# Moving the last third of a layer-norm statistics chain behind the next slab's score products on VectorE

## The chip, the cores and the metric

The kernel runs on the 8 cores of one Trainium2 chip, each with the same program on its own 4096 tokens; no core talks to another. Time is device microseconds of the slowest core.

## What is computed

One transformer layer over 4 sequences of 8192 tokens with 1024 features: an attention in which a token looks at itself and its two neighbours only (16 heads), a layer norm over input plus attention, a mixture of 8 experts of which each token weighs two, and a second layer norm. Cut to what matters here:

```python
xp = x @ Wp.T + bp                       # folded into Wq, Wk, Wv by the kernel
q, k, v = ...                            # 16 heads of 64
scores = einsum('bshd,bsnhd->bshn', q, kn)   # n: the 3 neighbours
attn = softmax(scores); out = einsum('bshn,bsnhd->bshd', attn, vn)
x = layernorm(x + out @ Wo.T + bo)       # (x - mean) / sqrt(var + eps)
x = layernorm(x + moe(x))                # 8 experts, top 2, relu squared
```

## The kernel before

Each core handles its tokens in three stages, one after the other. The first multiplies weight matrices together (to about 215 us). The second, attention and the first layer norm, runs over 8 slabs of 512 tokens (to about 1182 us). The third is the mixture of experts with the second layer norm (the rest). Data lies feature-major: 8 chunks (`dc`) of 128 features on the partitions, 512 tokens along the free axis.

The program is written as one instruction list per engine, with waits on counting semaphores set by hand (`p.wait(engine, semaphore, value)`). An engine executes its list strictly in order, so an instruction that waits holds back all that stand behind it on its engine. `_Prog.do` also puts a drain ahead of an instruction that touches a tile which an earlier one on the same engine has written since the last drain.

The loop over slabs calls these functions in this order (each puts work on several lists):

- `seg_scores(s)`: for each of the 8 chunks VectorE multiplies q with the three shifted k into three of six scratch slots (`pslots`; line 434, 24 products), and TensorE sums each over the features of a head (line 445, four matmuls for three slots, 32 in all). A slot can be written again only when the matmul that read it last is done, so VectorE can run six products ahead of TensorE, no more.
- `seg_softmax_a(s)`: ScalarE takes two exponentials (lines 454, 456); VectorE adds them (line 459).
- `seg_ln1_tail(s - 1)`: TensorE spreads the reciprocal deviation and the mean of the slab before over 128 partitions, reading `stb` (lines 623, 627); ScalarE copies both to slots 2 and 3 (lines 638, 640); VectorE normalises in 16 operations (lines 652, 657); SyncE stores the result.
- `seg_softmax_b(s)`: logarithm and exponential on ScalarE, two products on VectorE (lines 471, 473).
- `seg_qkv(s + 1)`: 384 matmuls (line 401), each group of eight copied out by ScalarE (line 407). Two PSUM banks take turns, so the third group waits for the first copy.
- `seg_wsum(s)`, `seg_wo(s)`: the weighted sum of v and the output projection (lines 493 to 559).
- `seg_ln1_stats_mm(s)`: sums of r1 and of its squares by matmuls with a column of ones (lines 572, 585).
- `seg_xt(s + 2)`: four input tiles are loaded by DMA from GpSimd's queue into two buffers (`xbt`), transposed by TensorE (line 340) and copied out by ScalarE (line 348); then a load of two halo rows and their transpose (line 364). The third and fourth load can start only when a buffer is free again, which is after the transposes of the first and second. This exists for s = 0 to 5.
- `seg_ln1_stats_tail(s)`: on one partition, VectorE computes mean and variance (lines 594 to 600); ScalarE takes the logarithm and the exponential that give 1/deviation (lines 605, 607); VectorE waits for that, multiplies it with the mean and casts both into `stb` (lines 610 to 614).

There is no `seg_qkv` after the scores of the last slab.

On ScalarE's list, lines 605 and 607 stand behind the copies of `seg_xt(s + 2)`. On VectorE's list, lines 610 to 614 stand ahead of the products of `seg_scores(s + 1)`. "Boundary" below is the stretch from the statistics of slab s to the start of `seg_qkv(s + 2)`; there are seven, and the first six hold a `seg_xt`.

Of the kernel before, what the change touches and what calls it, by code (L numbers as in the profile page):

```python
# [98 lines left out]
def build_program(T):  # L99
    assert T % SLAB == 0  # L100
    NSLAB = T // SLAB
# [37 lines left out]
    s_pe = semh("s_pe")  # L139
    s_dve = semh("s_dve")  # L140
    s_act = semh("s_act")
# [3 lines left out]
    p = _Prog(block)  # L145
# [174 lines left out]
    SS = {}  # L320
# [93 lines left out]
    def seg_scores(s):  # L414
        par = s % 2
        v_evac = SS[("evac", s)]
        ps_s[0].wait_writer(p)
        ps_s[2].wait_writer(p)
        si = 0
        vmm = 0  # L420
        for dc in range(NCH):
            prods = {}
            for o in (0, 1, 2):
                slot = si % 6
                si += 1
                scr = pslots[slot]
                if pslot_guard[slot] is not None:
                    p.wait("vector", *pslot_guard[slot])
                p.wait("vector", s_act, max(v_evac[(0, dc)], v_evac[(1, dc)]))
                vv = p.do("vector",  # L430
                          lambda En, o_=scr,
                          a=q_sb[:, par * PB + dc * XFW + 1: par * PB + dc * XFW + 513],
                          b=k_sb[:, par * PB + dc * XFW + o: par * PB + dc * XFW + o + 512]:
                          En.tensor_mul(o_, a, b),
                          reads=[_h(q_sb), _h(k_sb)], writes=[pslot_t[slot]], inc=s_dve)
                prods[o] = (slot, scr, vv)
            for bank, terms in ((ps_s[0], ((0, spk), (1, spkn))),
                                (ps_s[2], ((2, spk), (1, spkn)))):
                for j, (o, stat) in enumerate(terms):
                    slot, scr, vv = prods[o]  # L440
                    p.wait("tensor", s_dve, vv)
                    vmm = p.do("tensor",
                               lambda En, ot=bank.t, l=stat[:, dc * NH:(dc + 1) * NH], r=scr,
                               a=(dc == 0 and j == 0), b=(dc == NCH - 1 and j == 1):
                               En.matmul(ot[0:NH, :], l, r, start=a, stop=b),  # L445
                               inc=s_pe)
                    pslot_guard[slot] = (s_pe, vmm)
        SS[("scores", s)] = vmm

    def seg_softmax_a(s):  # L450
        p.wait("scalar", s_pe, SS[("scores", s)])
        p.wait("scalar", s_act, g_exp)
        p.wait("scalar", s_pe, g_mb)
        p.do("scalar", lambda En: En.activation(sm(0), ps_s[0].t[0:NH, :], AF.Exp),
             reads=[_h(ps_s[0].t)], writes=[_h(smt)], inc=s_act)
        v_e = p.do("scalar", lambda En: En.activation(sm(1), ps_s[2].t[0:NH, :], AF.Exp),
                   reads=[_h(ps_s[2].t)], writes=[_h(smt)], inc=s_act)
        p.wait("vector", s_act, v_e)
        v_sm = p.do("vector", lambda En: En.scalar_tensor_tensor(sm(2), sm(0), 1.0, sm(1), ALU.add, ALU.add),
                    reads=[_h(smt)], writes=[_h(smt)], inc=s_dve)  # L460
        SS[("v_sm", s)] = v_sm
        return v_e
# [127 lines left out]
    def seg_ln1_stats_tail(s):  # L590
        p.wait("vector", s_pe, SS[("v2s", s)])
        p.wait("vector", s_act, g_lnact)
        p.wait("vector", s_pe, SS.get("v_mb", 0))
        p.do("vector", lambda En: En.tensor_scalar_mul(sn(0), ps_s[1].t[0:1, :], 1.0 / D),
             reads=[_h(ps_s[1].t)], writes=[_h(stn)], inc=s_dve)
        p.do("vector", lambda En: En.tensor_scalar_mul(sn(1), ps_st.t[0:1, :], 1.0 / D),
             reads=[_h(ps_st.t)], writes=[_h(stn)], inc=s_dve)
        p.do("vector", lambda En: En.tensor_mul(sn(2), sn(0), sn(0)),
             reads=[_h(stn)], writes=[_h(stn)], inc=s_dve)
        v_var = p.do("vector", lambda En: En.tensor_sub(sn(1), sn(1), sn(2)),  # L600
                     reads=[_h(stn)], writes=[_h(stn)], inc=s_dve)
        ps_s[1].consumed(s_dve, v_var)
        ps_st.consumed(s_dve, v_var)
        p.wait("scalar", s_dve, v_var)
        p.do("scalar", lambda En: En.activation(sn(2), sn(1), AF.Ln, bias=LN_EPS),
             reads=[_h(stn)], writes=[_h(stn)], inc=s_act)
        v_rs = p.do("scalar", lambda En: En.activation(sn(1), sn(2), AF.Exp, scale=-0.5),
                    reads=[_h(stn)], writes=[_h(stn)], inc=s_act)
        p.wait("vector", s_act, v_rs)
        p.do("vector", lambda En: En.tensor_mul(sn(2), sn(0), sn(1)),  # L610
             reads=[_h(stn)], writes=[_h(stn)], inc=s_dve)
        p.do("vector", lambda En: En.tensor_copy(stb[:, 0:512], sn(1)),
             reads=[_h(stn)], writes=[_h(stb)], inc=s_dve)
        v_stb = p.do("vector", lambda En: En.tensor_copy(stb[:, 512:1024], sn(2)),
                     reads=[_h(stn)], writes=[_h(stb)], inc=s_dve)
        SS[("v_stb", s)] = v_stb
        return v_rs

    def seg_ln1_tail(s):
        par = s % 2  # L620
        p.wait("tensor", s_dve, SS[("v_stb", s)])
        ps_s[1].wait_writer(p)
        p.do("tensor", lambda En: En.matmul(ps_s[1].t[:], onescol[0:1, :],
                                            stb[0:1, 0:512], start=True, stop=True),
             inc=s_pe)
        ps_st.wait_writer(p)
        v_mb = p.do("tensor", lambda En: En.matmul(ps_st.t[:], onescol[0:1, :],
                                                   stb[0:1, 512:1024], start=True, stop=True),
                    inc=s_pe)
        SS["v_mb"] = v_mb  # L630
        p.wait("scalar", s_pe, v_mb)
        sbp = pslots[2]
        mbp = pslots[3]
        for sl in (2, 3):
            if pslot_guard[sl] is not None:
                p.wait("scalar", *pslot_guard[sl])
                pslot_guard[sl] = None
        p.do("scalar", lambda En: En.copy(sbp, ps_s[1].t[:]),
             reads=[_h(ps_s[1].t)], writes=[pslot_t[2]], inc=s_act)
        v_bb = p.do("scalar", lambda En: En.copy(mbp, ps_st.t[:]),  # L640
                    reads=[_h(ps_st.t)], writes=[pslot_t[3]], inc=s_act)
        ps_s[1].consumed(s_act, v_bb)
        ps_st.consumed(s_act, v_bb)
        pslot_guard[2] = (s_act, v_bb)
        pslot_guard[3] = (s_act, v_bb)
        p.wait("vector", s_act, v_bb)
        if rstg_free[par] is not None:
            p.wait("vector", *rstg_free[par])
        for dc in range(NCH):
            t0n = pslots[dc % 2]  # L650
            p.do("vector", lambda En, o=t0n, r=r1c(s, dc):
                 En.tensor_mul(o, r, sbp),
                 reads=[_h(q_sb), pslot_t[2]], writes=[pslot_t[dc % 2]], inc=s_dve)
            p.do("vector",
                 lambda En, o=r1n_stg[:, par * NCH * SLAB + dc * SLAB: par * NCH * SLAB + (dc + 1) * SLAB],
                 a=t0n:
                 En.tensor_sub(o, a, mbp),
                 reads=[pslot_t[dc % 2], pslot_t[3]], writes=[_h(r1n_stg)], inc=s_dve)
        g_r1n[par] = s_dve.n
        p.wait("sync", s_hw, s_hw.n)  # L660
        p.wait("sync", s_dve, s_dve.n)
        p.do("sync",
             lambda En, o=r1n_hbm.rearrange("p (c t) -> p c t", t=T)[:, :, s * SLAB:(s + 1) * SLAB],
             i_=r1n_stg[:, par * NCH * SLAB:(par + 1) * NCH * SLAB].rearrange("p (c t) -> p c t", t=SLAB):
             En.dma_start(out=o, in_=i_),
             inc=s_hw, inc_by=16)
        rstg_free[par] = (s_hw, s_hw.n)
# [3 lines left out]
    seg_xt(1)  # L671
    for s in range(NSLAB):
        seg_scores(s)
        v_e = seg_softmax_a(s)
        g_exp = v_e
        if s >= 1:
            seg_ln1_tail(s - 1)
        seg_softmax_b(s)
        if s + 1 < NSLAB:
            seg_qkv(s + 1)  # L680
        seg_wsum(s)
        seg_wo(s)
        seg_ln1_stats_mm(s)
        if s + 2 < NSLAB:
            seg_xt(s + 2)
        v_rs = seg_ln1_stats_tail(s)
        g_lnact = v_rs
        g_mb = s_pe.n
    seg_ln1_tail(NSLAB - 1)

    p.wait("gpsimd", s_pe, s_pe.n)
# [507 lines left out]
```

How the kernel before makes its waits and increments, by code:

```python
    def wait(self, eng, sem, val):  # L39
        if val <= 0:
            return
        self.ops[eng].append(lambda E, s=sem, v=val: E.wait_ge(s.h, v))
# [10 lines left out]
    def do(self, eng, fn, reads=(), writes=(), inc=None, inc_by=1):  # L53
        self._maybe_drain(eng, tuple(reads), tuple(writes))
        if inc is None:
            self.ops[eng].append(lambda E, f=fn: f(E))
        else:
            inc.n += inc_by
            self.ops[eng].append(lambda E, f=fn, s=inc, k=inc_by: f(E).then_inc(s.h, k))
        for h in writes:
            self.dirty[eng].add(id(h))
        for h in reads:
            self.read[eng].add(id(h))
        return inc.n if inc is not None else None
```

## Time and profile before

| | us |
|---|---|
| median of 2 runs | 3712.71 (3698.62 and 3726.8) |
| the profiled execution | 3500.52 |
| its span, slowest core (core 3) | 3499.0 |
| spans of the other cores | 3458.7 to 3491.5 |
| TensorE busy on core 3 | 2817.2 (81%) |
| VectorE busy | 1507.3 (43%) |
| ScalarE busy | 785.2 (22%) |

The profile is of one execution, on its slowest core. PE is TensorE, DVE VectorE, ACT ScalarE, POOL GpSimd, SP SyncE. "<-" in a wait names what ended it. The span runs from the first to the last instruction; the execution's time has 1.5 us more around it.

### The profile page before, as it was taken

What the parts mean: (1) busy time and instruction counts of PE and PEld (TensorE: products, weight loads), DVE (VectorE), ACT (ScalarE), POOL (GpSimd) and SP (SyncE); (2) the same over time, 40 slices, a digit from 0 to 9 for tenths busy, and PEclk for the clock granted to TensorE, in tenths of its full rate; (3) what the DMA queues carried; (4) which work ended last, traced back from release to release, by engine and by line L of the source; (5) the groups of instructions that cost most, each with busy time, mean ns of one, the idle gap of its engine ahead of it and who ended that gap; (6) DMA issues with size and microseconds to landing.
All of it is one profiled execution on the core that took longest, in us unless ns stands there. A gap on an engine that the chain in (4) does not pass through costs nothing.

```text
span 3499.0 us, 43503 instructions; the slowest of 8 cores (3458.7 to 3499.0 us)
## 1 busy us (share of the span) xinstructions
PE 2817.2 (81%) x13600; PEld 1300.6 (37%) x13600; DVE 1507.3 (43%) x2794; ACT 785.2 (22%) x1379; POOL 89.4 (3%) x127
## 2 busy tenths in 40 slices
PE   4578788878886399899967989987889996899992
PEld 1246344434442144344323434432334442344440
DVE  0001534353436344444554444455444455544445
ACT  1133344334433111111121111121111112111111
POOL 1000000000000000000000000000000000000000
PEclk9677888878887699999978999988999996999995
DMA  3420000100000335244324433432623523344431
GB/s 51 61 30 13 13 19 19 25 13 19 19 19 13 80 58 93 49 68 77 56 65 96 72 56 66 73 69 48 124 50 55 91 49 72 73 73 72 69 53 48
DMA packets 98764, 189.71 MB, mean 54 GB/s; under 512 B 3256, under 2 KB 11448, under 8 KB 98544
## 3 DMA queue, kind: packets, MB, share of 16 engines
q0 software_dynamic: 77744, 153.38, 27.0%
q1 hardware_dynamic: 20800, 33.56, 2.8%
q8 instruction: 119, 1.95, 0.2%
q14 instruction: 101, 0.83, 0.1%
HBM read 315.05 MB, written 25.17 MB: 97 GB/s over the span
## 4 chain that ended last, share of the span: by engine, by line
PE 52%; DMA 27%; DVE 8%; issue 5%; ACT 4%; DVEq 2%; ACTq 1%; POOLq 0%; POOL 0%; SPq 0%
PE ps_y L880 16%; PE ps_h L1055 15%; DMA w2e<-w 12%; DMA w1e<-w 11%; PE ps_mm L401 10%; PE ps_mm L551 3%; PE ps_f L225 3%; DMA xbt<-xs 2%; DVEq L49 2%; PE ps_s L445 2%; DVE y_acc L912 1%; ACTq L49 1%; ACT wbe L503 1%; ACT ln2scr L918 1%; DVE ln2t L992 1%
## 5 line engine op out<-in xcount | busy, mean ns | idle before, releaser
L880 PE MATMUL ps_y<-a_sb,w2e 128*128 128x512 bf16 x4096 | 915.6, 385 | 85.4 <-DMA w2e<-w 37.5
L1055 PE MATMUL ps_h<-r1n_ps,w1e 128*128 128x512 bf16 x4096 | 921.5, 386 | 56.9 <-DMA w1e<-w 47.5
L1062 ACT ACTIVATE t1u<-ps_h 128x512 bf16<-128x512 f32 x512 | 305.6, 597 | 1500.8 <-PE ps_h L1055 1453.2
L880 PEld LDWEIGHTS ps_y<-a_sb,w2e 128*128 128x128 bf16 x4096 | 402.8, 99 | 593.0 <-issue 131.2
L1055 PEld LDWEIGHTS ps_h<-r1n_ps,w1e 128*128 128x128 bf16 x4096 | 401.1, 99 | 564.1 <-issue 112.3
L892 DVE TENSOR_TENSOR y_acc<-y_acc,ps_y 128x512 f32<-128x512 f32 x448 | 307.8, 687 | 458.0 <-PE ps_y L880 456.5
L1067 DVE TENSOR_TENSOR t1u<-t1u,ps_gb 128x512 bf16<-128x512 bf16 x256 | 176.1, 688 | 258.1 <-ACT t1u L1062 256.0
L1067 DVE TENSOR_TENSOR t1u<-t1u,ps_b 128x512 bf16<-128x512 bf16 x256 | 176.1, 688 | 178.4 <-ACT t1u L1062 173.1
L1071 DVE TENSOR_TENSOR a_sb<-t1u 128x512 bf16<-128x512 bf16 x512 | 217.7, 425 | 47.7 <-issue 0.9
L225 PE MATMUL ps_f<-wxt_sb,wp_sb 128*128 128x512 bf16 x384 | 103.7, 443 | 84.7 <-DMA wxt_sb<-wqt 48.5
L551 PE MATMUL ps_mm<-k_sb,wot_sb 128*128 128x512 bf16 x512 | 141.6, 444 | 30.6 <-DVE pscr L522 24.2
L519 DVE TENSOR_TENSOR pscr<-wbe,v_sb 128x512 bf16<-128x512 bf16 x64 | 26.9, 420 | 266.8 <-ACT wbe L503 266.8
L401 PE MATMUL ps_mm<-x_fm,ckt 128*128 128x257 bf16 x1024 | 124.4, 284 | 14.2 <-ACT k_sb L407 13.6
L923 PE MATMUL ps_b<-ln2scr,onesv 128*1 128x512 bf16 x64 | 36.8, 576 | 108.1 <-ACT ln2scr L918 108.1
L401 PE MATMUL ps_mm<-x_fm,cvt 128*128 128x257 bf16 x1024 | 121.5, 281 | 0.5 <-ACT v_sb L407 0.2
L401 PE MATMUL ps_mm<-x_fm,cqt 128*128 128x257 bf16 x1024 | 119.1, 277 | 0.3 <-ACT q_sb L407 0.3
L401 PEld LDWEIGHTS ps_mm<-x_fm,ckt 128*128 128x128 bf16 x1024 | 97.5, 101 | 41.7 <-issue 19.3
L401 PEld LDWEIGHTS ps_mm<-x_fm,cvt 128*128 128x128 bf16 x1024 | 96.2, 100 | 24.6 <-issue 1.2
L401 PEld LDWEIGHTS ps_mm<-x_fm,cqt 128*128 128x128 bf16 x1024 | 94.0, 98 | 24.2 <-issue 0.5
L551 PEld LDWEIGHTS ps_mm<-k_sb,wot_sb 128*128 128x128 bf16 x512 | 56.0, 109 | 116.3 <-issue 71.9
L918 ACT CAST ln2scr<-y_acc 128x512 bf16<-128x512 f32 x64 | 39.5, 617 | 254.2 <-DVE y_acc L912 254.2
L225 PEld LDWEIGHTS ps_f<-wxt_sb,wp_sb 128*128 128x128 bf16 x384 | 42.0, 110 | 144.8 <-issue 139.3
(153 smaller groups left out, 1678.6 us busy)
## 6 DMA issues: line engine op xcount, KB each, us to landing
w1e<-w POOLq DMA_DIRECT2D x32, 2048.0 KB, 15.0
w2e<-w POOLq DMA_DIRECT2D x32, 2048.0 KB, 15.2
out<-otok SPq DMA_DIRECT2D x8, 2048.0 KB, 7.2
xbt<-xs POOLq DMA_DIRECT2D x32, 256.0 KB, 3.9
r1n_hbm<-r1n_stg SPq DMA_DIRECT2D x8, 1024.0 KB, 5.2
r1n_ps<-r1n_hbm SPq DMA_DIRECT2D x4, 2048.0 KB, 21.6
wp_sb<-wp POOLq DMA_DIRECT2D x1, 2048.0 KB, 17.1
wxt_sb<-wqt POOLq DMA_DIRECT2D x1, 2048.0 KB, 17.9
```

Source lines behind the costliest of these rows:

```text
L49: self.ops[eng].append(lambda E: E.drain())
L225: En.matmul(o[:], l, r, start=a, stop=b),
L401: En.matmul(o[:, 0:w_], l, r, start=a, stop=b),
L445: En.matmul(ot[0:NH, :], l, r, start=a, stop=b),
L551: En.matmul(o[:], l, r, start=a, stop=b),
L880: En.matmul(o[:], l, r, start=a, stop=b),
L892: va = p.do("vector", lambda En, o=ydst, i_=role.t: En.tensor_add(o, o, i_[:]), reads=[_h(role.t), _h(y_acc)], writes=[_h(y_acc)], inc=s_dve)
L918: vc = p.do("scalar", lambda En, o=rb, i_=ydst: En.copy(o, i_), reads=[_h(y_acc)], writes=[_h(ln2scr)], inc=s_act)
L1055: En.matmul(o[:], l, r, start=a, stop=b),
L1062: va = p.do("scalar", lambda En, o=t1, i_=role.t: En.activation(o, i_[:], AF.Relu), reads=[_h(role.t)], writes=[_h(t1u)], inc=s_act)
L1067: p.do("vector", lambda En, o=u, a=t1, gb_=gbank.t: En.tensor_mul(o, a, gb_[:]), reads=[_h(t1u), _h(gbank.t)], writes=[_h(t1u)], inc=s_dve)
L1071: a=u, b=t1: En.tensor_mul(o, a, b),
```

## The change

`seg_ln1_stats_tail` is cut in two. Its first part ends after the two ScalarE instructions. The second part, `seg_ln1_stats_tail_b`, holds VectorE's wait for them and the three VectorE instructions that form `stb`. It is called after `seg_scores` of the next slab, so on VectorE's list the wait and the three instructions now stand behind the 24 products and ahead of line 459. After the last slab both parts follow each other as before. The new part repeats a wait on the matmuls that last read `stb`. Nothing moves on the lists of TensorE, ScalarE, GpSimd and SyncE.

```diff
--- before.py
+++ after.py
@@ -606,7 +606,12 @@
              reads=[_h(stn)], writes=[_h(stn)], inc=s_act)
         v_rs = p.do("scalar", lambda En: En.activation(sn(1), sn(2), AF.Exp, scale=-0.5),
                     reads=[_h(stn)], writes=[_h(stn)], inc=s_act)
-        p.wait("vector", s_act, v_rs)
+        SS[("v_rs", s)] = v_rs
+        return v_rs
+
+    def seg_ln1_stats_tail_b(s):
+        p.wait("vector", s_act, SS[("v_rs", s)])
+        p.wait("vector", s_pe, SS.get("v_mb", 0))
         p.do("vector", lambda En: En.tensor_mul(sn(2), sn(0), sn(1)),
              reads=[_h(stn)], writes=[_h(stn)], inc=s_dve)
         p.do("vector", lambda En: En.tensor_copy(stb[:, 0:512], sn(1)),
@@ -614,7 +619,6 @@
         v_stb = p.do("vector", lambda En: En.tensor_copy(stb[:, 512:1024], sn(2)),
                      reads=[_h(stn)], writes=[_h(stb)], inc=s_dve)
         SS[("v_stb", s)] = v_stb
-        return v_rs
 
     def seg_ln1_tail(s):
         par = s % 2
@@ -671,6 +675,8 @@
     seg_xt(1)
     for s in range(NSLAB):
         seg_scores(s)
+        if s >= 1:
+            seg_ln1_stats_tail_b(s - 1)
         v_e = seg_softmax_a(s)
         g_exp = v_e
         if s >= 1:
@@ -686,6 +692,7 @@
         v_rs = seg_ln1_stats_tail(s)
         g_lnact = v_rs
         g_mb = s_pe.n
+    seg_ln1_stats_tail_b(NSLAB - 1)
     seg_ln1_tail(NSLAB - 1)
 
     p.wait("gpsimd", s_pe, s_pe.n)
```

## Rows read from the trace of the kernel before

**Rows 1.** the page's head, the slowest core

```profile
span 3499.0 us, 43503 instructions; the slowest of 8 cores (3458.7 to 3499.0 us)
```

**Rows 2.** busy time by stretch: from, to, length, each engine, TensorE clock, DMA, GB/s

```profile
398.00:1182.00 784.00, 596.59 (x3517) 318.15 (x3515) 341.57 (x761) 294.16 (x546) 14.75 (x28) 0.81 0.09 18
...
1182.00:1800.00 618.00, 530.04 (x2340) 228.87 (x2340) 284.04 (x507) 103.02 (x171) 17.17 (x20) 0.93 0.42 74
```

**Rows 3.** TensorE's waits, 280 to 1180 us: us in total, times, longest

```profile
PE ps_s L445 <- DVE pscr L434: 30.2, 7, 7.0
...
PE ps_mm L401 <- ACT k_sb L407: 13.6, 8, 1.9
```

**Rows 4.** VectorE's waits, 280 to 1180 us

```profile
DVE stn L610 <- ACT stn L607: 72.2, 8, 12.6
```

**Rows 5.** timeline around the second slab boundary: start, duration, instruction, [idle before]

```profile
518.54 0.68 DVE L600 TENSOR_TENSOR stn<-stn 1x512 f32<-1x512 f32 x1
...
528.32 0.35 PE L364 MATMUL ps_tb<-idb,xh 2*128 2x2 bf16 x8 [1.57 <-DMA xh<-xs]
...
529.59 0.63 ACT L607 ACTIVATE stn<-stn 1x512 f32<-1x512 f32 x1
530.37 0.68 DVE L610 TENSOR_TENSOR stn<-stn 1x512 f32<-1x512 f32 x1 [11.15 <-ACT stn L607]
...
531.65 0.41 DVE L614 CAST stb<-stn 1x512 bf16<-1x512 f32 x1
531.99 1.78 DVE L434 TENSOR_TENSOR pscr<-q_sb,k_sb 128x512 bf16<-128x512 bf16 x4
...
532.54 0.59 PE L445 MATMUL ps_s<-pscr,spk_sb 128*16 128x512 bf16 x1 [3.88 <-DVE pscr L434]
...
541.52 0.94 DVE L434 TENSOR_TENSOR sqscr<-q_sb,k_sb 128x512 bf16<-128x512 bf16 x2
...
543.13 0.39 PE L623 MATMUL ps_s<-stb,onescol 1*128 1x512 bf16 x1
...
544.56 0.56 ACT L638 CAST pscr<-ps_s 128x512 bf16<-128x512 f32 x1
544.77 0.68 DVE L459 SCALAR_TENSOR_TENSOR smt<-smt 16x512 bf16<-16x512 bf16 x1 [2.31 <-ACT smt L456]
...
546.92 1.01 ACT L407 ACTIVATE k_sb<-ps_mm,cbk 128x257 bf16<-128x257 f32 x2
...
547.52 12.73 PE L401 MATMUL ps_mm<-x_fm,ckt 128*128 128x257 bf16 x112 [1.92 <-ACT k_sb L407]
```

**Rows 6.** stretches inside that boundary, columns as in rows 2

```profile
532.50:537.00 4.50, 4.46 (x11) 1.43 (x12) 3.98 (x11) 0.00 (x0) 0.53 (x1) 0.50 0.41 57
537.00:543.50 6.50, 6.17 (x25) 1.84 (x22) 4.90 (x13) 0.10 (x1) 0.00 (x0) 1.00 0.01 1
```

**Rows 7.** timeline around the seventh boundary, VectorE, then TensorE

```profile
1100.56 0.68 DVE L610 TENSOR_TENSOR stn<-stn 1x512 f32<-1x512 f32 x1 [1.58 <-ACT stn L607]
...
1102.18 1.78 DVE L434 TENSOR_TENSOR pscr<-q_sb,k_sb 128x512 bf16<-128x512 bf16 x4
...
1116.14 0.42 DVE L652 TENSOR_TENSOR pscr<-q_sb,pscr 128x512 bf16<-128x512 bf16 x1 [0.51 <-ACT pscr L640]
...
1102.73 0.58 PE L445 MATMUL ps_s<-pscr,spk_sb 128*16 128x512 bf16 x1 [6.99 <-DVE pscr L434]
...
1125.78 0.58 PE L493 MATMUL ps_s<-wpl,bpk_sb 16*128 16x512 bf16 x1 [11.86 <-DVE wpl L473]
```

**Rows 8.** what TensorE's score products waited for on core 0: us, times

```profile
  DVE pscr L434: 30.4, 8
```

**Rows 9.** POOL's load issues at the second boundary, timeline

```profile
521.85 0.53 POOL L160 DMA_DIRECT2D xbt<-xs  x1 [4.11 <-DMA xbt<-xs]
...
533.68 0.53 POOL L160 DMA_DIRECT2D xbt<-xs  x1 [4.13 <-PE ps_s L445]
```

## The prediction

> **What bounds the kernel now.** I read the page first, to know the size of the whole: a span of 3499.0 us on the slowest core [rows 1], 1.5 us less than that execution's own time of 3500.5 us. Then the busy time by stretch [rows 2]. The reader should see that the attention stage of the loop, 398 to 1182 us, is 784 us long with TensorE busy for 596.6, while the expert stage behind it keeps TensorE busy for 530 of 618 us in its first stretch. The change touches only the attention stage, and there only the places between slabs; all else can only be shifted.
>
> Next the waits of that stage. TensorE's list has one wait that names VectorE's score products: 30.2 us in 7 times, one of them 7.0 [rows 3]. VectorE's has one wait that names the second ScalarE instruction of the statistics: 72.2 us in 8 times [rows 4]. The two are linked, and the timeline of one boundary shows how [rows 5]. VectorE ends line 600 at 518.54 + 0.68 = 519.22 us. It then idles 11.15 us until ScalarE ends line 607. ScalarE is late because its list holds the copies of the next transposes first, and these wait for loads. TensorE ends the last of those transposes at 528.32 + 0.35 = 528.67 us and stands 3.87 us, until the first product arrives for the matmul at 532.54. So what sets the end there is first the loads, up to 528.67, and then a tail in series: lines 605, 607, 610, 612, 614, one product. Only the tail can be taken off. The other five boundaries with a transpose stage repeat this: (30.2 - 7.0) / 6 = 3.87 us each. The 11.15 us of VectorE's idling are no measure of the gain, since TensorE is busy with loads and transposes for most of them.
>
> **What is removed: the six full boundaries.** After the change VectorE goes from 519.22 us straight to the products. Their inputs (q and k of the next slab) were made before the weighted sum, and the slots are free. All 24 took 541.52 + 0.94 - 531.99 = 10.47 us, 0.436 us each [rows 5]. Six fill the slots by about 521.9; VectorE then waits for TensorE, which arrives at 528.67. The first score matmul starts there: 3.87 us earlier.
>
> Does the head start of six products bring more? Before, the last product ended 542.46 - 532.54 = 9.92 us after the first matmul. After, the seventh product needs the first matmul done, the eighth the fourth, and so on round the slots. TensorE issued 11 matmuls in the first 4.5 us, 0.41 each, at a granted clock of 0.50, the lower level of 1.2 GHz, and was at 1.00 after that [rows 6]. Walking the slots at this pace, the thirteenth product starts about 4.65 us after the first matmul, and the last ends 12 x 0.436 = 5.2 later, at 9.9 us. The head start is used up by the slow clock, so I take 0. If the clock rose at once, 18 products from 0.75 us on would end at 8.6: 1.3 us more gain. If it rose a little later than before, some 0.4 less.
>
> **What is added behind the scores.** The three instructions took from 530.37 to 531.65 + 0.41 = 532.06, 1.69 us. They now stand behind the last product. VectorE stood idle there for 2.31 us before line 459 [rows 5], so on VectorE itself they are hidden, with 0.6 us to spare; the wait for line 607 ahead of them is long over (529.59 + 0.63 = 530.22). But `stb` is late next. TensorE's line 623 started 543.13 - 542.46 = 0.67 us after the last product; now it must wait until 0.05 + 1.69 + 0.1 = 1.84 us after it, 1.17 us more, and line 627, the whole of `seg_qkv` and, by line 638, ScalarE are queued behind it. ScalarE's line 638 started 2.10 us after the last product because two exponentials were ahead of it. Now line 627 starts at 1.84 + 0.22 and takes as long as line 623's 0.39, which with some 0.15 of signalling gives 2.6: ScalarE is 0.5 us late, and with it lines 640, 466, 468 and the copy of line 407. TensorE's own 1.17 us mostly vanish, since after 16 matmuls it waited 1.92 us for that copy anyway until 547.52 [rows 3, 5]. Net loss 0.5 us a boundary; bounds 0 (if signalling is quicker) and 1.17 (if nothing absorbs it).
>
> A full boundary gains 3.87 - 0.5 = 3.4 us, bounds 3.87 - 0.4 - 1.17 = 2.3 and 3.87 + 1.3 = 5.2. Six: 20.2 us (14 to 31).
>
> **The seventh boundary** has no transposes. VectorE idled 1.58 us before line 610 and spent 1102.18 - 1100.56 = 1.62 until the first product [rows 7]. Both leave the path, less about 0.1: 3.1 us. TensorE's 6.99 us become 3.9. No projection follows there: the path goes by VectorE's 16 normalising operations from 1116.14 to TensorE's 11.86 us wait that ends at 1125.78, and the first of the 16 waits for ScalarE's copies, late by the same 0.5. Gain 2.6 us (1.9 to 3.1). The last slab's tail is unchanged.
>
> **Sum.** 20.2 + 2.6 = 22.8 us, bounds 16 and 34. Against the profiled execution, 3500.5 - 22.8 = 3477.7. The median of the two runs shown is 3712.7, 212 us above the profiled execution; nothing in the trace says where these lie. The gain is made of VectorE and ScalarE durations, which do not follow TensorE's clock, so I take it off unchanged: 3712.7 - 22.8 = **3689.9 us**, a gain of 0.6%. Core 0 shows the same wait, 30.4 us [rows 8], so the slowest core has no special position.
>
> **The loads.** The products now run while loads are in flight. At 521.85 POOL found its load landed after 4.11 us, which ran beside one-partition work; the load whose landing it awaited until 533.68 took 4.13, beside lines 610 to 614 and four products [rows 9]. I take 0 for it. The Trainium skill speaks against the change here: the page SBUF — State Buffer, section on who interferes with whom, says VectorE and GpSimd share ports under an exclusive lock, and a load issued from GpSimd stalls while VectorE holds it. By that rule the loads would come later by up to the six products; by the row nothing moves.
>
> **The rivals.**
> - *The loads are stretched by the products.* Place: the tile load issued about 517.2. Price: at most the six early products, 2.6 us a boundary, 15.6 us over six. The sum becomes 7 us: 3705.5. Against it the two equal landings; for it, that they are a thin sample. Chance 0.13.
> - *The change does nothing that counts.* Another wait keeps the products where they are, a slot or a late q, or the gain is lost before the projection. Then TensorE's wait stays at 3.87 and the time at 3712.7. The slots' last readers and the copies of q are done long before, so 0.04.
> - *Slower: the clock stays low into the projection.* TensorE starts on the scores after 12 us of sparse transposes, and now meets a second pause of 1.2 us at line 623. Before, the clock had risen 4.5 us into the scores and was 1.00 ahead of the projection [rows 6]. If it stayed at 0.50, each microsecond of the projection's work would take one more. 3.4 us of such work in each boundary cancels the gain, and that is where it decides; 5 us cost 6 x 1.6 = 10 us net of it: 3722. Being 2% slower takes (74 + 23) / 7 = 14 us of it each time. Against it: the 1.92 us pause at 547.52 did not bring the clock down before. Chance 0.07.
>
> **From these to the numbers.** The forecast holds 0.76. The two runs shown lie 14 us either side of their median, and the expert stage's mean clock of 0.93 [rows 2] moves it: 0.01 of it over 2317 us, TensorE busy for 86%, is some 21 us, as much as the whole gain and with no sign of its own. The range goes from the upper bound of the gain less both runs' distance (3712.7 - 34 - 28 = 3651) to the slower rival and a little over it, 3725. About 2% is what a measurement of this kernel can tell from no change, 74 us. No case of the profile reaches that; I leave 0.04 for faster and 0.03 for slower, and 0.93 within.
>
> **What the profile after would show.** VectorE's wait at line 610 falls from 72.2 us to nearly the last slab's 1.6. VectorE's waits at line 434 on TensorE grow instead, by about 7.5 us (521.9 to 528.67 + 0.75) in each of six boundaries. TensorE's wait at line 445 falls from 30.2 to about 4, all in the seventh. TensorE gains a wait at line 623, 7 times 1.2 us, and its wait at line 401 for line 407 shrinks from 1.9 to about 1.3. Scores end about 3.9 us sooner after the transposes. Landing times of the loads stay at 4 us. The prediction is wrong if these landings grow, if the scores end no earlier, or if the first projection matmuls show a clock of 0.50.

## The result

| | before | after |
|---|---|---|
| median, us | 3479.7 (10 runs, 3475.0 to 3749.3) | 3454.1 (11 runs, 3448.8 to 3640.1) |
| ratio | | 0.9927, 95% interval 0.9916 to 0.9939 |
| first to last line 600, us (7 slabs) | 768.3 (core 3), 767.6 (core 7) | 744.0 (core 7) |

The change takes 0.73% off, 25 us (21 to 29). Some executions of either kernel are 4 to 8% longer than the rest, with a lower granted clock on one half of the cores or on both; the ratio compares the shorter ones alone, and the two runs shown ahead of the prediction were both of the longer kind. With the eight runs measured later the median before is 233 us lower. The third row is my yardstick for the attention stage below: from the start of line 600 (the last of VectorE's four statistics operations, whatever number it has in a kernel) in the first slab to the same in the last. It holds all seven boundaries and nothing of the first and last stage. It fell by 23.6 us on core 7 (by 19.9 to 25.0 on the eight cores, core by core), against a forecast of 22.8 for the whole.

The waits of TensorE after the change (slowest core, core 7, same stretch as rows 3, same columns):

```profile
PE ps_tb L340 <- DMA xbt<-xs: 47.5, 12, 4.8
...
PE ps_s L627 <- DVE stb L619: 14.7, 8, 6.8
...
PE ps_mm L401 <- ACT k_sb L407: 10.3, 8, 2.2
...
PE ps_s L445 <- DVE pscr L434: 3.7, 1, 3.7
```

The reader should hold the last line against the first of [rows 3]: 30.2 us in seven waits have become 3.7 in one, which is the seventh boundary. The new line is the wait for `stb`; 6.8 us of it belong to the last slab and were there before, so the change added 7.9 us in seven waits, 1.1 each. Part of that came back: the wait for ScalarE's copy went from 13.6 to 10.3 us. The first line is no gain of the change: core 7 lies some 24 us earlier in its span than core 3 did before, so the stretch cuts off two waits of the first slabs; from 240 us on both kernels wait 55.4 us for tiles, 14 times. VectorE's wait that was 72.2 us [rows 4] is now this (core 7):

```profile
DVE stn L615 <- ACT stn L607: 1.7, 1, 1.7
```

The second boundary in the timeline (core 7, columns as in rows 5, whose lines these answer):

```profile
490.80 0.68 DVE L600 TENSOR_TENSOR stn<-stn 1x512 f32<-1x512 f32 x1
491.41 1.78 DVE L434 TENSOR_TENSOR pscr<-q_sb,k_sb 128x512 bf16<-128x512 bf16 x4
...
501.10 0.35 PE L364 MATMUL ps_tb<-idb,xh 2*128 2x2 bf16 x8 [1.78 <-DMA xh<-xs]
501.44 0.58 PE L445 MATMUL ps_s<-pscr,spk_sb 128*16 128x512 bf16 x1
...
502.20 0.42 DVE L434 TENSOR_TENSOR pscr<-q_sb,k_sb 128x512 bf16<-128x512 bf16 x1 [8.16 <-PE ps_s L445]
...
510.42 0.94 DVE L434 TENSOR_TENSOR sqscr<-q_sb,k_sb 128x512 bf16<-128x512 bf16 x2
...
511.28 0.67 DVE L615 TENSOR_TENSOR stn<-stn 1x512 f32<-1x512 f32 x1
...
512.55 0.41 DVE L619 CAST stb<-stn 1x512 bf16<-1x512 f32 x1
...
513.21 0.37 PE L627 MATMUL ps_s<-stb,onescol 1*128 1x512 bf16 x1 [1.12 <-DVE stb L619]
...
514.00 0.58 ACT L642 CAST pscr<-ps_s 128x512 bf16<-128x512 f32 x1 [0.45 <-PE ps_st L631]
...
516.98 12.73 PE L401 MATMUL ps_mm<-x_fm,ckt 128*128 128x257 bf16 x112 [1.31 <-ACT k_sb L407]
```

VectorE now goes from the statistics to the products without a pause and then stands 8.16 us because its slots are full. TensorE starts the scores with no idle at all behind the last transposes. The last product ends at 511.36, 9.92 us after the first score matmul, exactly as before the change. `stb` then costs what it was to cost: line 627 starts 1.85 us after the last product (0.67 before), line 642 (638 before) 2.64 (2.10 before), and the projection goes on 5.62 us after it (5.06 before).

A table that no single view gives: the time from TensorE's first matmul of one kind to its first of the next, from its timeline, mean over the six full boundaries. It carries most of what follows, so the kernels measured later stand in it too. "Transposes" runs from the first transpose to the first score matmul, with the waits for the loads in it; weighted sum and output projection (wo) are means over the last seven slabs. Each kernel stands with its slowest core, but warm2_after with core 4, since on its cores 2 and 3 the clock was low in the projection (774.9 and 782.7 us in the last column). The cores of one execution differ by up to 9.4 us in the last column, mostly in wo; where that matters, all eight are given.

| kernel | transposes | scores | projection | weighted sum | wo | first to last line 600 |
|---|---|---|---|---|---|---|
| before | 17.1 | 11.3 | 45.5 | 17.6 | 20.1 | 768.3 |
| changed | 13.5 | 12.4 | 44.9 | 17.6 | 19.8 | 744.0 |
| early | 13.2 | 11.3 | 45.6 | 17.6 | 19.8 | 740.6 |
| dbl | 12.7 | 14.0 | 45.9 | 17.6 | 19.3 | 754.2 |
| warm2_after | 13.3 | 10.9 | 45.0 | 17.9 | 18.5 | 728.2 |
| port_mul | 13.1 | 12.6 | 45.0 | 17.6 | 20.0 | 744.9 |
| port_copy | 13.7 | 12.2 | 45.0 | 17.6 | 19.7 | 743.9 |
| bufs4_before | 8.8 | 11.4 | 45.6 | 17.6 | 18.7 | 709.6 |
| bufs4_after | 4.5 | 11.9 | 44.9 | 18.0 | 18.5 | 681.3 |
| bufs4_early | 7.2 | 11.2 | 45.6 | 18.0 | 19.5 | 704.3 |
| bufs4_after_wo | 4.5 | 11.8 | 45.0 | 18.6 | 16.7 | 674.0 |

Before to changed, for one full boundary: 3.6 us less ahead of the scores, 1.1 more in them (TensorE's wait for `stb` counts there), 0.6 less in the projection. The seventh boundary gave 3.3 us in its statistics stage (11.5 to 8.2). Nothing shows that the few tenths in the wo stage are the change's doing; what sets its length is a finding of its own, below.

### The profile page after: what moved, and what is told of

Same layout as the page of the kernel before. It is cut to its first block, busy times and chain, and to the rows that moved or that the text cites. A ratio compares the mean times of both kernels' runs of the same rounds, so it can differ in the third digit from the quotient of the medians.

```text
span 3449.2 us, 43503 instructions; the slowest of 8 cores (3353.9 to 3449.2 us)
## 1 busy us (share of the span) xinstructions
PE 2790.8 (81%) x13600; PEld 1287.7 (37%) x13600; DVE 1507.4 (44%) x2794; ACT 785.7 (23%) x1379; POOL 89.4 (3%) x127
## 4 chain that ended last, share of the span: by engine, by line
PE 53%; DMA 27%; DVE 8%; issue 5%; ACT 4%; DVEq 2%; ACTq 1%; POOLq 0%; POOL 0%; SPq 0%
PE ps_y L887 16%; PE ps_h L1062 15%; DMA w2e<-w 12%; DMA w1e<-w 10%; PE ps_mm L401 10%; PE ps_mm L551 3%; PE ps_f L225 3%; DMA xbt<-xs 2%; DVEq L49 2%; PE ps_s L445 2%; DVE y_acc L919 1%; ACT wbe L503 1%; ACT ln2scr L925 1%; ACTq L49 1%; DVE ln2t L999 1%
## 5 line engine op out<-in xcount | busy, mean ns | idle before, releaser
L225 PE MATMUL ps_f<-wxt_sb,wp_sb 128*128 128x512 bf16 x384 | 90.7, 401 | 85.2 <-DMA wxt_sb<-wqt 48.7
L401 PE MATMUL ps_mm<-x_fm,ckt 128*128 128x257 bf16 x1024 | 118.8, 275 | 10.9 <-ACT k_sb L407 10.3
L434 DVE TENSOR_TENSOR pscr<-q_sb,k_sb 128x512 bf16<-128x512 bf16 x128 | 51.5, 422 | 140.0 <-PE ps_s L445 71.5
## 6 DMA issues: line engine op xcount, KB each, us to landing
wp_sb<-wp POOLq DMA_DIRECT2D x1, 2048.0 KB, 17.4
```

The source lines that it names most:

```text
L225: En.matmul(o[:], l, r, start=a, stop=b),
L401: En.matmul(o[:, 0:w_], l, r, start=a, stop=b),
```

## The experiments

The edits are shown shortened, in part in words.

**early: the late stb taken away.**

```diff
 seg_xt(s + 2), on ScalarE's list
     copy of transposed tile 0, copy of tile 1
+    lines 605, 607 (logarithm, exponential) here
     copy of tile 2, copy of tile 3, halo copy
 VectorE, boundaries 1 to 6
+    tail_b ahead of the products, seventh boundary behind them
```

> The changed kernel with ScalarE's two statistics instructions moved ahead of its third transpose copy, where ScalarE stands idle for a load anyway, and VectorE's last three instructions back ahead of the products (the seventh boundary stays as changed). It takes away the cost that the prediction put at 0.5 us a boundary, late stb, and keeps the 3.87. Theory: TensorE's wait for stb goes from 14.7 us to the last slab's 6.8 plus about 1, its wait at the score products stays near 4 us (the seventh boundary alone), and the time from the first to the last line 600 falls from 744.0 to 741 us; ratio 0.992. Rival (moving the chain off ScalarE's list is all that counts, or the 0.5 us was never paid): 744 us, ratio 0.993. Rival on the other side (VectorE now starts its products 3.3 us later, at about 522.5 in the second boundary's time, and that is too late for TensorE): over 745 us.

Measured: 740.6 us, ratio 0.9924 (0.9906 to 0.9942). The interval of the whole kernel can't tell 0.9924 from 0.9927; the stage table can. The scores stage gives back its 1.1 us and the projection takes 0.7 again: 0.4 us a boundary (3.4 us in all by the yardstick), for which the prediction had 0.5. In the medians over the eight cores of each kernel the scores stage gives back 1.4, so 0.7 net; the price of the late stb lies between 0.4 and 0.7 us. TensorE's waits on core 3, the one for stb almost wholly the last slab's again:

```profile
PE ps_s L633 <- DVE stb L625: 8.0, 2, 6.8
...
PE ps_s L447 <- DVE pscr L436: 3.7, 1, 3.7
```

The first product starts later than in the changed kernel, yet TensorE did not wait for it: while the loads last, where VectorE does its three instructions is free.

**dbl: the late stb made later.**

```diff
 def seg_ln1_stats_tail_b(s):
     p.wait("vector", s_act, SS[("v_rs", s)])
     p.wait("vector", s_pe, SS.get("v_mb", 0))
+    if s < NSLAB - 1:
+        two tensor_mul of 1x512 fp32 on a scratch tile
```

> The changed kernel with two more one-partition products (0.68 us each and a drain, together 1.54 us, results unused) ahead of line 615 in the moved part, at the seven boundaries. It doubles the one cost that the prediction added. Theory (late stb is now on the path by way of ScalarE's copies, with nothing left to absorb more of it): the whole 1.54 us is paid at each boundary, 7 x 1.54 = 10.8 us, 744.0 becomes 755 us, ratio 0.996; TensorE's wait for stb grows by 10.8 us. Rival (it hides behind ScalarE and the 0.7 us that VectorE still idles): 744 to 750 us, ratio 0.993 to 0.994.

Measured: 754.2 us against 744.0, ratio 0.9970 (0.9958 to 0.9983), which is 15 us above the changed kernel; TensorE's wait for stb 24.3 us, 9.6 more than in the changed kernel. At its own place the lateness is paid almost in full: in the medians over eight cores the scores stage is 1.45 us longer, and at the seventh boundary the time from the scores to the weighted sum is 1.5 longer, 10.2 us in all of the 10.8 forecast. The total is not so clean. Core by core it grew by 2.3 to 10.2 us: wo was shorter here (18.6 us in the median over the cores, 19.7 in the changed kernel) while the projection was longer in some slabs. The start of one such projection (core 0), then the same one in the changed kernel (core 7), columns as in rows 2:

```profile
967.68:972.58 4.90, 4.02 (x25) 2.81 (x25) 2.60 (x7) 3.16 (x6) 0.00 (x0) 0.64 0.00 0
```

```profile
964.57:969.47 4.90, 3.59 (x32) 2.96 (x32) 3.28 (x8) 3.63 (x7) 0.00 (x0) 1.00 0.00 0
```

This is the prediction's third rival, the clock low into the projection, and it appears when TensorE stands 2.49 us for stb in the place of 1.12: 19 of the 48 projections (six boundaries, eight cores) are 0.9 to 2.4 us longer than the changed kernel's median at the same boundary and 11 more are 0.2 to 0.6 longer, while the changed kernel's own 48 spread by less than 0.3 us. The change stayed clear of it by less than 1.4 us of waiting. With `early` this gives the shape: the first 1.2 us of lateness cost 0.4 to 0.7, because ScalarE's two exponentials and TensorE's wait for ScalarE's copy cover the rest; beyond that nearly all is paid, and in some slabs a slow projection comes on top.

**port_mul and port_copy: do the loads feel VectorE?**

```diff
 seg_scores(s), 1 <= s <= 6, after the sixth product
+    13 x tensor_mul(dmb, cqt[:, 0:512], ckt[:, 0:512])       # port_mul
+     8 x tensor_copy(dmy[:, 0:1024], dmy[:, 1024:2048])      # port_copy, fp32
```

> The changed kernel with VectorE kept busy after its sixth product by 13 more products of two on-chip bf16 tiles (0.52 us each with the drain, results unused), so that it works through the loads of the fourth tile and the halo rows instead of standing idle. Theory (the loads do not feel VectorE): TensorE's waits for xbt and xh stay at 55 and 14 us in all and POOL sees each load land after 4.0 to 4.3 us. Rival (the lock between VectorE and GpSimd's descriptor writing): landings longer by 0.5 to 2 us, the waits 10 to 20 us longer.

> The same with 8 copies of 1024 fp32 elements in the place of the 13 products: single-source copies, the form that the Trainium skill (SBUF, State Buffer, section on who interferes with whom) names as the one that locks GpSimd out. Theory (loads do not feel VectorE): landings 4.0 to 4.3 us, as with the products. Rival (that rule): each copy holds the port for its whole duration, descriptors are written only between copies, and the landings of the fourth tile and the halo rows grow by 1 to 3 us, TensorE's waits by 10 to 30 us in all.

Measured: 744.9 and 743.9 us. From 240 us on, TensorE's waits for tiles and for halo rows are 52.9 and 14.8 us with products (55.4 and 14.6 in the changed kernel on core 7): nothing. With copies they are 55.4 and 15.9, and the issue itself changed. GpSimd's load issues in the view of line 160, first the changed kernel (core 7), then port_copy (core 2; durations as min/median/max ns, then the first and the last start):

```profile
L160 POOL DMA_DIRECT2D xbt<-xs x32: 528/528/557, 198.4 to 944.6; - x32
...
L160 POOL DMA_DIRECT2D xh<-xs x8: 511/511/522, 216.2 to 949.4; - x8
```

```profile
L160 POOL DMA_DIRECT2D xbt<-xs x32: 528/530/988, 195.8 to 941.6; - x32
...
L160 POOL DMA_DIRECT2D xh<-xs x8: 517/682/918, 214.1 to 946.4; - x8
```

The second boundary of port_copy in VectorE's and then in GpSimd's timeline (core 2):

```profile
490.84 6.18 DVE L428 COPY dmy<-dmy 128x1024 f32<-128x1024 f32 x8
```

```profile
490.65 0.99 POOL L160 DMA_DIRECT2D xbt<-xs  x1 [3.77 <-DMA xbt<-xs]
```

An issue that falls among the copies takes up to 0.99 us in the place of 0.53. That fits the lock of which the Trainium skill speaks (SBUF — State Buffer, section on who interferes with whom): copies can shut GpSimd out, while products of two tensors do not hold up a load. Both agree here: no issue among port_mul's took over 0.56 us on any core. The lock costs 0.1 to 0.5 us an issue, not the 1 to 3 that the rival had for a landing, and the time did not follow. So the first rival of the prediction, loads stretched by the products, is out: the change's products do not do it (a tile lands after 3.8 us in the median with and without the change, on core 7), and even the worse form would cost a few tenths.

**warm_before, warm_after, warm2_after: is the head start eaten by the slow clock?** Filler matmuls into a PSUM bank that the scores overwrite later; the numbers are per wait (third tile, fourth tile, halo).

```diff
 seg_xt(s), s >= 2, on TensorE's list ahead of the wait for the load
+    fill(8), fill(7), fill(3)        # warm_*: matmuls 128x512 of idb and cqt
+    fill(14), fill(16), fill(7)      # warm2_after
```

> The changed kernel with filler matmuls on TensorE (8, 7 and 3, results unused) ahead of the waits for the third tile, the fourth tile and the halo rows in the six boundaries that have transposes; they fit into waits of 4.3, 3.6 and 1.7 us. It tests the step that the six products of head start are worth nothing because TensorE reads the scores at the lower clock. Theory (slow clock eats the head start): the score matmuls start at a granted clock of 1.00, the last product ends 8.6 us after the first score matmul instead of 9.9, and the kernel is 6 x 1.3 = 8 us faster than the changed kernel, a ratio of about 0.990 to the kernel before. Rival (VectorE and the slots set the pace whatever the clock): last product still 9.9 us after the first matmul, ratio 0.993. Second rival (fillers get in the way of the transposes): slower than the changed kernel by up to 1 us a boundary.

> The kernel before with the same filler matmuls. Without the change no product is made ahead, and VectorE paces the scores from its first product on at 0.436 us each. Theory: no gain from the clock, ratio 1.000 (within 0.001), TensorE's wait at line 445 stays 3.9 us a boundary. Rival (the clock by itself is worth something, by the transposes or the scores): 0.5 to 1 us a boundary, ratio 0.998 to 0.999.

The first pair decided nothing on the question. In warm_after (core 6) the fillers ran at the full clock but left pauses of 1.33, 2.18 and 1.10 us at the second boundary, and the clock was down to 0.50 again when the scores began; the first ten score matmuls were 0.43 us apart as before, and the attention stage took 744.2 us, as without fillers. Its ratio, 0.9903 (0.9863 to 0.9943), is too wide to say more. warm_before gave 767.4 us and 0.9986 (0.9974 to 0.9998): no gain in the attention stage; the 0.1% in the whole is not explained.

> The changed kernel with more filler matmuls (14, 16 and 7 in the place of 8, 7 and 3). In the first try the fillers ran at the full clock and left pauses of 1.3, 2.2 and 1.1 us, and the scores still began at the lower clock, so it said nothing on the head start. These fill the waits almost wholly. Theory (the slow clock eats the head start): the score matmuls start 0.22 us apart, the last product ends 8.6 us after the first score matmul instead of 9.9, and the time between the first and the last one-partition subtraction (line 600 of the changed kernel) falls from 744.0 by 6 x 1.3 to 736 us; ratio 0.990. Rival (the slots and VectorE set the pace at any clock): 9.9 us and 744 us. Second rival (the fillers run over the landings): TensorE reaches the scores later, over 746 us.

Measured: 728.2 us, ratio 0.9863 (0.9844 to 0.9882). Stretches around the second boundary, columns as in rows 2; first the changed kernel (core 7), the first stretch ahead of the scores, then two in them, then warm2_after (core 4), cut alike:

```profile
497.00:501.40 4.40, 1.31 (x16) 1.07 (x16) 0.00 (x0) 1.01 (x1) 0.51 (x1) 0.50 0.12 20
501.40:505.90 4.50, 4.50 (x13) 1.50 (x12) 2.24 (x6) 1.34 (x3) 0.55 (x1) 0.50 0.42 58
505.90:512.50 6.60, 5.87 (x22) 1.73 (x20) 5.81 (x15) 0.20 (x1) 0.53 (x1) 0.99 0.32 40
```

```profile
491.00:496.00 5.00, 4.26 (x33) 1.96 (x30) 0.00 (x0) 1.01 (x1) 0.51 (x1) 1.00 0.31 50
496.00:500.50 4.50, 4.20 (x23) 1.53 (x20) 3.09 (x9) 1.34 (x3) 0.55 (x1) 1.00 0.42 61
500.50:506.40 5.90, 4.68 (x16) 1.28 (x15) 5.26 (x14) 0.59 (x1) 0.53 (x1) 1.00 0.30 45
```

With the clock at 1.00, 17 score matmuls fit into the first 4.5 us in the place of 11 (the counts in the rows hold some transposes too), VectorE makes 9 products there instead of 6, and the last product ended 8.51 us after the first score matmul: 8.6 had been worked out, 9.92 is the value at the slow clock. Without the head start the full clock would bring nothing by the prediction's rows, since 24 products take VectorE 10.47 us; no run has that pair. The scores stage fell from 12.4 to 10.9 us, 6 x 1.5 = 9 us in all. Most of the remaining 7 us sits in the wo stage (19.8 to 18.5, seven times, less 0.3 that the weighted sum is longer), which no expectation had, and which the fillers are not shown to cause: on cores 4 to 7 wo is 18.5 to 19.3 us and the last column 727.3 to 733.5.

**Four input buffers.** The loads set the boundary's end up to 528.67 us in the prediction's own reading. This takes them away, with and without the change, and with the early pair.

```diff
-    xbt = psb("xbt", [128, 2 * 1024], BF16)
+    xbt = psb("xbt", [128, 4 * 1024], BF16)
-    tb = xbt[:, (tt % 2) * 1024:(tt % 2) * 1024 + 1024]
+    tb = xbt[:, tt * 1024:tt * 1024 + 1024]        # xtile_free likewise by tt
```

> The kernel before with four tile buffers for the input instead of two, so that all loads of a boundary are issued a slab earlier. The change is not in it. Theory: loads set the end of the boundary up to 528.7 and lines 605 to 614 in series after them; without the loads ScalarE's four copies end near 520.8, and the series then ends at 524.8 instead of 532.5: 7.7 us a boundary, 46 us in all, ratio 0.987. TensorE's waits for xbt and xh fall from 55 and 14 us to those of the first two slabs. Rival (the transposes then wait for something else, PSUM banks or the halo load): 3 to 5 us a boundary, ratio 0.992 to 0.995.

> The changed kernel with the same four buffers. Theory: the change is worth more here, since the loads no longer hide VectorE's head start: first product at 519.3 in the second boundary's time against about 524.3, less 0.5 for late stb: 4.5 us a boundary beyond bufs4_before, 27 + 3 us in all; ratio 0.978. Rival (the gain of the change is tied to the loads, and with them gone ScalarE's chain is short enough): bufs4_before and bufs4_after within 5 us, ratio 0.986.

> Both, four buffers and the early ScalarE pair. Without the waits for loads ScalarE has no idle time ahead of its third copy: it would wait there for line 600 (519.2), and the two remaining copies and the products come later. Theory: first product near 522.4 instead of 519.3, slower than bufs4_after by 2 to 3 us a boundary, 12 to 18 us, ratio 0.982 to 0.983. Rival (taking late stb away is worth its 0.5 us whatever the loads do): 3 us faster than bufs4_after.

> The changed kernel with four input buffers once more, in five rounds, for its ratio to the kernel before: its profiled run showed 681.3 us between the first and the last line 600 against 709.6 for four buffers without the change and 744.0 for the change alone. Theory: 768.3 - 681.3 = 87 us less than before in the attention stage, all of it kept to the end, ratio 0.975. Rival (the expert stage gives part back): 0.980 or more.

From 240 us on TensorE waits for no input load any more, in bufs4_before and in bufs4_after. Measured: bufs4_before 709.6 us, ratio 0.9813 (0.9792 to 0.9834); bufs4_after 681.3 us, and run again 681.5 us with the ratio 0.9730 (0.9717 to 0.9744); bufs4_early 704.3 us, 0.9807 (0.9761 to 0.9852). A boundary of bufs4_before (core 3), then one of bufs4_after (core 6):

```profile
468.82 1.07 PE L340 MATMUL ps_tb<-idb,xbt 128*128 128x128 bf16 x16
...
476.75 0.41 DVE L614 CAST stb<-stn 1x512 bf16<-1x512 f32 x1
477.09 1.78 DVE L434 TENSOR_TENSOR pscr<-q_sb,k_sb 128x512 bf16<-128x512 bf16 x4
477.64 0.59 PE L445 MATMUL ps_s<-pscr,spk_sb 128*16 128x512 bf16 x1 [4.32 <-DVE pscr L434]
```

```profile
466.50 1.07 PE L340 MATMUL ps_tb<-idb,xbt 128*128 128x128 bf16 x16
...
469.74 1.77 DVE L434 TENSOR_TENSOR pscr<-q_sb,k_sb 128x512 bf16<-128x512 bf16 x4
470.65 0.35 PE L364 MATMUL ps_tb<-idb,xh 2*128 2x2 bf16 x8 [0.48 <-ACT x_fm L348]
470.99 0.58 PE L445 MATMUL ps_s<-pscr,spk_sb 128*16 128x512 bf16 x1
```

Without the change, the loads gone, TensorE still waits 4.32 us for the tail in series (3.87 with two buffers). With it, that wait is gone too: the scores start 4.5 us after the first transpose instead of 8.8. So the change is worth 709.6 - 681.3 = 28.3 us here (30 forecast) against 24.3 on two buffers: its gain does not hang on the loads. bufs4_before beat its own forecast, 58.7 us less than before in place of 46: 6 x 8.3 = 50 in the transposes, the rest in wo (20.1 to 18.7). bufs4_early shows that a place which was free beside the loads is not free without them: the pair on ScalarE pushes its third and fourth copy back, transposes take 7.2 us instead of 4.5, and the kernel loses 23 us to bufs4_after (12 to 18 forecast; wo is 7 of the 23). `early` had gained 3.4.

**bufs4_after_wo: the clock at the output projection.** The stage table left one column unexplained: wo took 17.4 to 18.1 us in some slabs and 19.0 to 20.7 in others. The granted clock was 0.50 at the start of all of them; it rose 2.3 to 3.9 us into the short ones and 7.0 to 9.5 us into the long ones (all slabs and cores of all kernels above, of warm2_after cores 4 to 7). Two stages of bufs4_after (core 6), of 19.0 and of 17.5 us, each in its first 4.9 us and the next, columns as in rows 2:

```profile
443.07:447.97 4.90, 4.11 (x10) 1.37 (x10) 3.52 (x8) 0.62 (x2) 0.00 (x0) 0.50 0.00 0
447.97:452.87 4.90, 4.90 (x20) 1.95 (x19) 1.45 (x3) 0.00 (x0) 0.00 (x0) 0.79 0.00 0
...
545.72:550.62 4.90, 4.11 (x13) 1.46 (x13) 3.64 (x8) 0.62 (x2) 0.00 (x0) 0.66 0.00 0
550.62:555.52 4.90, 4.90 (x24) 2.19 (x23) 1.92 (x3) 0.00 (x0) 0.00 (x0) 1.00 0.01 2
```

Which of the two a slab gets differs between the cores of one execution; why is not shown. So a difference of 1 us in wo between two kernels may be chance.

```diff
 seg_wsum, TensorE, chunks 2 to 7, ahead of the first of three matmuls
+    fill(2)
 seg_wo, TensorE, ahead of its first matmul
+    fill(8)
```

> The changed kernel with four input buffers and filler matmuls (results unused) in the weighted sum: 2 ahead of the first of three matmuls in six of its eight chunks and 8 ahead of the output projection. It asks where the gains come from that the boundary does not explain: in the stage table the output projection takes 17.4 to 17.9 us in some slabs and 19.3 to 20.6 in others, and its first 4.9 us run at a granted clock of 0.55 after a weighted sum at 0.54. Theory (the clock at its start decides): all eight projections take about 17.5 us instead of 17.7 to 20.1 in bufs4_after, while the weighted sum, whose pace VectorE sets, stays at 17.5 to 18.3; 6 to 10 us less, ratio 0.970 to 0.971 against 0.973. Rival (the fillers delay the real matmuls, VectorE is starved): the weighted sum grows by 2 us or more a slab, and the kernel is no faster than bufs4_after, ratio 0.973 or more. Second rival (the difference in the projection is not the clock at its start): lengths stay mixed.

Measured: wo 16.8 to 17.2 us in the first seven slabs and 15.4 in the last, the weighted sum 18.1 to 18.7 (20.0 in the last, the fillers included), 674.0 us, ratio 0.9675 (0.9647 to 0.9703; 0.970 to 0.971 forecast). The start of the stage, first in the changed kernel (core 7), then here (core 0, with the weighted sum ahead of it); the 0.55 of the expectation was read 3.95 us further on:

```profile
576.14:581.05 4.91, 4.11 (x10) 1.44 (x11) 3.50 (x9) 1.00 (x2) 0.00 (x0) 0.50 0.00 0
```

```profile
525.30:542.80 17.50, 16.70 (x42) 3.67 (x42) 13.60 (x34) 13.59 (x25) 0.00 (x0) 0.61 0.00 0
542.80:547.70 4.90, 3.22 (x15) 1.35 (x14) 3.53 (x8) 0.53 (x1) 0.00 (x0) 1.00 0.02 3
```

In this slab the clock is at 1.00 from the stage's first matmul; in the eight slabs of core 0 it rises 0 to 2.4 us into the stage, and all eight are short. So when the clock rises is what makes a wo stage long or short. In the medians over the eight cores wo takes 2.1 us less than in bufs4_after, for 1.1 more in the weighted sum. This is the fastest kernel of the study, 3.3% below the kernel before and 2.5% below the changed one by their ratios (0.9675 / 0.9927 = 0.975).

## Why the prediction was right or wrong

**Wrong: the base.** The step that failed is the last of the sum, "I take it off unchanged: 3712.7 - 22.8". The median of two runs was taken as the time from which the changed kernel would be measured, although the same paragraph had the profiled execution 212 us below and no reason for the gap. Over ten runs the kernel before has its median at 3479.7 us, and 3454 lies far under the range's 3651. Taken from the profiled execution, the same sum gives 3477.7, 24 us above what was measured, since that execution itself was 21 us slower than the later median. The trace could have told that much: core 3, its slowest, reached the first line 600 only at 401.9 us, core 7 at 377.8, with a mean granted clock of 0.76 against 0.85 up to 377 us. So the slowest core did have a special position, though not in the boundaries. The range was built from effects inside the kernel and the 14 us between two runs. Two values and one that contradicts both are no measure of scatter; the range had to include 3478. The 2% that the prediction gave as what a measurement can tell was too coarse: the interval of the ratio is 0.12% to either side.

**Right: the gain.** 22.8 us forecast, bounds 16 and 34; 25 (21 to 29) by the ratio, 23.6 by the trace (core 7). Step by step:

| step | forecast, us | measured, us |
|---|---|---|
| VectorE's wait, line 610 (now 615) | 72.2 to about 1.6 | 1.7 |
| TensorE's wait at line 445 | about 4, seventh boundary | 3.7, once |
| last product after first score matmul | 9.9 | 9.92 |
| the same at the full clock | 8.6 | 8.51 (warm2_after) |
| line 627 after the last product | 1.84 | 1.85 |
| ScalarE's line 642 after it | 2.6 | 2.64 |
| new wait for stb, seven times | 1.2 | 1.1 |
| wait for ScalarE's copy at line 401 | 1.3 | 1.31 |
| net cost of late stb, a boundary | 0.5 | 0.56 (5.62 - 5.06), 0.4 to 0.7 (early) |
| median landing of a tile load | 4 | 3.8 (3.8 before, core 7) |
| VectorE's first wait for a slot | 7.5 | 8.16 |

The last row is off because in that execution the loads took 0.5 us longer after line 600, not because of a step.

**What the sum left out.** The stages of the six full boundaries give 6 x 3.1 = 18.6 us (20.2 forecast) and the seventh 3.3 - 0.1 = 3.2 (2.6 forecast; the late `stb` cost it 0.1 us and not 0.5): 22. Most of the 2.5 us up to the 24.3 between the two slowest cores lies in the wo stage, by the clock, and belongs to no step of the prediction. That it is the change's doing is not shown.

**The rivals.** Loads stretched by the products: excluded by port_mul, with four buffers the change is worth no less. The prediction let the Trainium skill (SBUF — State Buffer, section on who interferes with whom) speak for this rival, which misread it: the same section says that products of two tensors did not hold up a load. Nothing that counts: excluded by the transposes column of the stage table, 17.1 to 13.5. The clock low into the projection: it was at 1.00 there, as before, and the prediction's own row for the scores held, 0.50 in the first 4.5 us and 0.99 after; but dbl shows that this rival was near, for with 1.5 us more of lateness it came true in 19 of 48 projections.

## What to carry to other kernels

An engine's wait is worth moving as far as another engine is released by it: here 72 us of VectorE's idling held 30 us of TensorE's, and some 24 came off. Work moved behind something else must be followed to the next reader in order; about half of the first microsecond of lateness was covered, and of the next 1.5 us nearly nothing. And before a gain of 1% is taken off a time, ask which of the times in hand is the usual one, for that can be off by more than the gain.

## What the runs showed of the hardware

- TensorE's clock is worth some 16 us in this stage, 9 in the scores and 7 in the output projections, next to the 24 us of the change. In the kernel before and in the changed one it is at 0.50 when the scores of the full boundaries and the output projections begin, after sparse work. Matmuls with unused results in the pauses held it at 1.00 up to the scores and took 1.5 us off a scores stage whose products had a head start; ahead of the output projection they brought its rise forward, and took some 2 us off it at 1 us more in the weighted sum. The Trainium skill (TensorE: Matmul & The Clock Gate, section on why this matters for your kernels) warns of idle gaps between bursts of matmuls. The runs agree that gaps bring the clock down, and show that short ones suffice: between bursts at the full clock, pauses of 1.33, 2.18 and 1.10 us ended at 0.50, and 18 fillers a boundary gave nothing (744.2 us), where 37 kept it at 1.00.
- One pause can tip it: with a wait of 2.49 us ahead of the projection (dbl) 19 of 48 projections were 0.9 to 2.4 us longer, the clock at 0.64 in the first 4.9 us of the one shown; with 1.12 us none was over 0.3 us longer.
- The clock's fall costs a head start. Six products made ahead were worth 0 at the lower clock and 1.4 us at the full one.
- An fp32 copy on VectorE makes a load issue on GpSimd up to 0.46 us longer (0.99 for 0.53); products of two bf16 tiles leave it alone.
